# An AdaLN block with attention and routed LoRA experts: a VectorE order, a TensorE order, and the second half of the FFN in float16 pairs

## What is computed

```python
h = _layernorm(x) * (1 + ca) + sa
x = x + ga * attention(h, Wq, Wk, Wv, Wo)
h = _layernorm(x) * (1 + cb) + sb
top_w, top_i = top_k(h @ gate_w.T, 2);  routing = softmax(top_w)
# for every expert e, with its weight w_e per token:
h1 = h @ w1.T + h @ A1.T @ B1.T * 2;  h3 = h @ w3.T + h @ A3.T @ B3.T * 2
act = silu(h1) * h3
out += w_e * (act @ w2.T + act @ A2.T @ B2.T * 2)
x = x + gb * out
```

## Time and profile before

| | us |
|---|---|
| median of 3 runs | 527.52 |
| the profiled execution's own time | 527.2 |
| its span, first to last instruction | 525.2 |
| mean granted TensorE clock | 0.987 of 2.4 GHz |
| TensorE busy | 467.9 (89%) |
| VectorE / ScalarE / GpSimd busy | 355.4 / 331.5 / 278.2 |

### The profile page before, as it was taken

One profiled execution on the slowest core, in us unless ns is written; L12 is line 12 of the kernel. 1 busy time (PEld: TensorE's weight loads), 2 busy tenths in 40 slices (PEclk: granted clock), 3 DMA queues, 4 the chain that ended last, 5 costly groups with the idle time before them and its releaser, 6 DMA issues.

```text
span 525.2 us, 11947 instructions
## 1 busy us (share of the span) xinstructions
PE 467.9 (89%) x4424; PEld 320.3 (61%) x4424; DVE 355.4 (68%) x1016; ACT 331.5 (63%) x592; POOL 278.2 (53%) x208
## 2 busy tenths in 40 slices
PE   3777789989999999999999988989798979999996
PEld 3363566667767677777677766767663534564444
DVE  3686667777777778777878887888648746424442
ACT  3417889888789878888888889797435443001110
POOL 4136698894779875769999557631103204001110
PEclk9978999999999999999999999999999989999999
DMA  8156043394352584343536413342110000010001
GB/s 302 49 143 217 24 130 94 119 222 93 102 89 64 163 149 117 99 74 110 168 87 141 112 21 112 101 116 41 21 21 1 1 0 1 0 41 1 0 2 40
DMA packets 58169, 44.47 MB, mean 85 GB/s; under 512 B 36608, under 2 KB 50432, under 8 KB 58112
## 3 DMA queue, kind: packets, MB, share of 16 engines
q1 hardware_dynamic: 56624, 41.60, 31.3%
q10 hardware_dynamic: 1488, 2.10, 1.1%
HBM read 23.77 MB, written 11.53 MB: 67 GB/s over the span
## 4 chain that ended last, share of the span: by engine, by line
PE 65%; DVE 12%; ACT 11%; issue 7%; POOL 2%; DMA 1%; SPq 0%; ACTq 0%; DVEq 0%; POOLq 0%
PE ps L463 10%; PE ps L389 8%; PE ps L391 8%; PE ps L390 8%; ACT prob L777 6%; PE ps L714 4%; PE ps L481 4%; PE ps L447 4%; PE ps L445 4%; PE ps L485 4%; PE ps L483 4%; PE ps L652 3%; PE ps L642 3%; DVE pl L1061 2%; ACT rot L756 1%
## 5 line engine op out<-in xcount | busy, mean ns | idle before, releaser
L777 ACT ACTIVATE prob<-prob,least 128x512 f32<-128x512 f32 (+3 forms) x256 | 131.5, 551 | 0.0
L1053 DVE CUSTOM_DVE_ANT_0 prob<-ps,causal 128x512 f32<-128x512 f32 (+3 forms) x256 | 114.3, 484 | 4.9 <-PE ps L447 4.3
L463 PE MATMUL ps<-ident,prob 128*128 128x128 f32 x640 | 93.4, 279 | 23.2 <-ACT prob L777 18.6
L784 ACT ACTIVATE ph<-ps 128x512 f16<-128x512 f32 (+1 forms) x128 | 89.5, 700 | 28.4 <-PE ps L463 25.0
L1061 DVE SCALAR_TENSOR_TENSOR pl<-ps,ph 128x512 f16<-128x512 f32 (+1 forms) x128 | 99.0, 815 | 0.0
L463 PEld LDWEIGHTS ps<-ident,prob 128*128 128x128 f32 x640 | 67.8, 141 | 38.0 <-ACT prob L777 25.7
L445 PE MATMUL ps<-kT_h,qT 128*128 128x512 f16 (+3 forms) x256 | 76.6, 300 | 4.5 <-DVE least L1053 2.9
L1314 POOL TENSOR_TENSOR on_l<-on,on_h 128x512 f16<-128x512 f32 x32 | 37.1, 1160 | 63.6 <-ACT on_h L791 63.6
L447 PE MATMUL ps<-kT_l,qT 128*128 128x512 f16 (+3 forms) x256 | 69.8, 300 | 0.0
L481 PE MATMUL ps<-vh,ph 128*128 128x65 f16 x640 | 64.9, 194 | 0.9 <-DVE pl L1061 0.9
L483 PE MATMUL ps<-vl,ph 128*128 128x64 f16 x640 | 64.9, 193 | 0.0
(11 more groups left out here) (156 smaller groups left out, 951.8 us busy)
## 6 DMA issues: line engine op xcount, KB each, us to landing
spill<-rot SPq DMA_DIRECT2D x20, 512.0 KB, 3.4
qT<-spill SPq DMA_DIRECT2D x16, 512.0 KB, 3.6
wst<-chunks SPq DMA_DIRECT2D x30, 256.0 KB, 3.9
kT_h<-spill SPq DMA_DIRECT2D x8, 256.0 KB, 4.0
oT<-wmod ACTq DMA_DIRECT2D x3, 512.0 KB, 11.4
kT_l<-spill SPq DMA_DIRECT2D x4, 256.0 KB, 4.8
out<-xs SPq DMA_DIRECT2D x4, 256.0 KB, 2.1
w_h<-w2T SPq DMA_DIRECT2D x1, 640.0 KB, 6.1
```

The costliest lines, as they stand in the source:

```text
L463: mm = pe.transpose(ps[:, PT_BANK + c // 512, c % 512:c % 512 + P], prob[:, m % 2, c:c + P], ident[:, :])
L777: act.activation(prob[:, m % 2, c], prob[:, m % 2, c], ACT.Exp, bias=least[:, m % 2, qt:qt + 1], scale=-1.0).then_inc(exp_done, 1)
L1053: ins = dve.tensor_tensor_reduce(prob[:, m % 2, at:at + w], ps[:, bank, off:off + w], causal[:, S - w:S], -1.0 / HD ** 0.5, 3.0e38, ALU.ad ...
```

## The change

Attention, per period:
- VectorE does `probs_low(n+1, 0)` before `norm(n)` instead of behind `row_max` 2; part 1 stays last.
- TensorE does `scores(n+3, 0)` before the output product and before the second projection step; group 1 stays last.

FFN:
- A2, w2 and B2 come as five float32 chunks of 512 columns (period 54, into `raw` and `rot`), and are split like the other weights: five ScalarE copies in periods 57 to 61 (`late_high`), five GpSimd subtractions one period later (`late_low`).
- `z_product` becomes three float16 matmuls per tile and choice, one tile later; ScalarE rounds `av` (`products_high`), GpSimd makes the remainder (`products_low`; the last one is VectorE's). `av` gets two slots.
- `gsum` is rounded by ScalarE (`sums_high`), its remainder made by GpSimd (`sums_low`); w2 and B2 products are three float16 matmuls each. In batch 0 the w2 products stand behind tile 5 of batch 0, their B2 part in tile 1 of batch 1; in batch 1 two thirds of the w2 products stand before the last `z_product`.
- ScalarE takes SiLU of the next tile's first choice before it rounds the second product of this one.
- The masks' PSUM banks alternate (`i % 2`).
- Batch 1: the residual moves to GpSimd in four pieces, the inverse root and the normalisation to GpSimd, the transposes from tile 1 to tile 2, logits from 1 to 3, choices, weights and masks a tile or more later.

```diff
                 if n == 54:
-                    sp.wait_ge(proj_done, len(TILES))
-                    ... four DMAs: a2, w2
+                    lowered(sp, len(ITEMS) - 1)
+                    for i in range(LATE_CHUNKS):
+                        sp.dma_start(late_stage(i), chunks[N_CHUNKS + i]).then_inc(ld_late, 16)
 # TensorE, period n
+                if n + 3 < HEADS:
+                    scores(n + 3, 0)
                 if n >= 10 and n % 2 == 0:
...
                     output((n - 10) // 8, (n - 10) % 8 // 2, out_bank(n))
                 for step in steps[1:]:
                     project(step)
-                for f in range(2):
-                    if n + 3 < HEADS:
-                        scores(n + 3, f)
+                if n + 3 < HEADS:
+                    scores(n + 3, 1)
 # VectorE, period n
+                if 0 <= n + 1 < HEADS:
+                    probs_low(n + 1, 0)
                 if n >= 0:
                     norm(n)
...
                 if 0 <= n + 1 < HEADS:
-                    probs_low(n + 1, 0)
                     probs_low(n + 1, 1)
 # TensorE, FFN
-                mm = pe.matmul(ps[:, 4 + s, :], a2_sb[0:m, f, :], av[0:m, s, :], start=(f == 0), stop=(f == FT - 1))
+                    mm = mm3(ps[:, 4 + s, :], a2_h[0:m, f, :], a2_l[0:m, f, :], av_h[0:m, i % 2, s, :], av_l[0:m, i % 2, s, :],
+                             f == 0, f == FT - 1)
+            def w2_product(b, t, f):
+                m, at = min(P, F - f * P), t % 2 * D
+                pe.wait_ge(fs["gl"], b * FT + f + 1)
+                for l, r in ((gsum_h, w2_h), (gsum_h, w2_l), (gsum_l, w2_h)):
+                    mm = pe.matmul(ps[:, 6 + t // 2, at:at + D], l[0:m, f, c], r[0:m, f, :], ...)
+            def b2_product(b, t):
+                pe.wait_ge(fs["ul"], 1 if b == 0 else 2 + t // 2)
+                for l, r in ((u_h, b2_h), (u_h, b2_l), (u_l, b2_h)):
...
             for b in range(B):
                 for f in range(FT):
                     if f < FT - 1:
                         if b > 0 or f > 0:
                             h_base(b, f + 1)
-                        h_lora(b, f + 1)
-                        if b == 0 and f == 1:
+                            h_lora(b, f + 1)
+                        if b == 0 and f == 2:
                             pe.wait_ge(op_added, 4 * W + 4)
                             ... transposes of batch 1
+                        if b == 0 and f == 3:
+                            gate_logits(1)
                     elif b == 0:
                         h_base(1, 0)
-                        h_lora(1, 0)
+                    else:
+                        pe.wait_ge(fs["og"], 2)
+                        w2_products(1, (0, 1))
                     h_second(b, f)
+                    if b == 0 and f == 4:
+                        mask_transposes(1, (0, 1))
                     if f > 0:
-                        z_product(b, f - 1, 1)
-                    z_product(b, f, 0)
+                        z_product(b, f - 1)
+                    if b == 1 and f == 1:
+                        for t in range(T):
+                            b2_product(0, t)
...
+                w2_products(b, (2, 3))
+                z_product(b, FT - 1)
+                w2_products(b, (4, 5))
 # ScalarE, FFN, tile i
+                if i > 0:
+                    sums_high(i - 1)
+                if i == 1:
+                    root(1, B + 2)
+                products_high(i, 0)
+                if i == 2:
+                    modulate_ffn(1, 6)
...
+                silu(i, 1)
+                if i < B * FT - 1:
+                    silu(i + 1, 0)
+                products_high(i, 1)
 # GpSimd, FFN, tile i
+                products_low(i, 0)
                 if i == 1:
+                    inverse_root(1)
+                    for t in range(T):
+                        normalise(1, t)
+                sums(i)
+                if i < B * FT - 1:
+                    products_low(i, 1)
...
+                sums_low(i)
```

365 lines of the change are left out of this document (222 added, 143 removed).

## The result

| | before | after |
|---|---|---|
| median, us | 527.94 (4 runs) | 519.57 (4 runs) |
| ratio, 95% interval | | 0.9857, 0.9828 to 0.9886 |
| the profiled execution's own time | 527.2 | 520.1 |
| its span | 525.2 | 518.2 |
| mean granted clock | 0.987 | 0.972 |

The changed kernel is faster by 1.4% by the ratio (about 7.5 us), by 8.4 us by the medians; the forecast was 515.4 us, 4.2 us less. The time lies in the forecast's range of 508.5 to 521.5 us, but the gain is under the 2% that it called a clear one, and for which it gave 0.62. (One of the four runs of before, 563.66 us, was disturbed and is left out of the ratio.)

What follows compares the result with a forecast made beforehand. TensorE was taken as the main bound, busy 467.9 of 525.2 us, with ScalarE's queue and later VectorE among the heads. 527.2 + 1.0 (attention) - 6.9 (batch 0) - 6.9 (batch 1) + 1.0 (end) = 515.4 us, range 508.5 to 521.5.

Steps and rivals of the forecast that it cites:

- Heads, VectorE's order: Attention: the low part moved ahead of the normalisation shortens TensorE's waits for `pl` from 310 us on, -3.3 us.
- (a): Attention, periods 50, 52, 54, 56: the moved scores fill TensorE's output-product waits for the normalisation, -1.7 us.
- (b): Attention, periods 3, 7, ..., 47: scores between two steps of one tile cost 0.43 us each of twelve times, +5.2 us.
- Rival A: Attention: the path through period 35 has unseen slack, so (b) costs nothing, 510.2 us; chance 0.25.
- (c): Attention: output products end 0.43 us later; VectorE's idle time hides it, uncovered up to 0.43 us per odd period.
- Late weights: Attention, periods 57 to 61: five ScalarE roundings ahead of the tile-1 exponential cost a quarter of 3.1 us, +0.8 us.
- FFN, matmul time: FFN, both batches: float16 z products -5.2 us, w2 and B2 products -9.0 us, together -14.2 us.
- FFN, batch 0's waits: FFN of batch 0: TensorE's idle stretches in the new order sum to 9.4 us instead of 7.1, +2.3 us.
- The clock dip: FFN of batch 0: half of the 1.6 us lost at the low clock is given back, -0.8 us.
- B: FFN of batch 0: GpSimd's and ScalarE's queues hold TensorE 4 us more, with a second dip 520.5 us; chance 0.15.
- D: FFN, both batches: removed matmul time returns as uncovered waits, 522.5 us with half given back; chance 0.10.
- C: FFN: GpSimd becomes the bound, deciding from 7.5 us a tile, at worst +35, 550 us; chance 0.05.

Runs made afterwards that it cites:

- experiment 1: Three edits of the changed kernel that undo or restrict its new orders among the heads: attn_old 518.05 us, dve_old 521.86 us, pe_even 512.62 us.
- pe_even: Changed kernel with the first half of the scores ahead of the output product in even periods only, in odd ones behind the projection step: 512.62 us, ratio 0.9735.
- dve_old: Changed kernel with only VectorE's order among the heads put back, both low parts behind the normalisation: 521.86 us, ratio 0.9914.
- attn_old: Changed kernel with both TensorE's and VectorE's order among the heads put back, late weights and FFN as changed: 518.05 us, ratio 0.9847.
- best_late: best with ScalarE's late-weight roundings behind the tile-1 exponential instead of ahead of it in periods 57 to 61: 505.52 us, ratio 0.9602.
- experiment 2: Cost of low-clock stretches: changed kernel with zero-adding matmuls in three TensorE waits of batch 0, 520.58 us; the changed kernel unedited again, 519.18 us.
- experiment 4: Changed kernel with GpSimd subtracting batch 1's product remainders twice or three times instead of once: 524.88 and 538.04 us.
- best: pe_even plus two ScalarE/VectorE reorderings in batch 0, an early four-column SiLU, and product (4,0) ahead of batch 1's second choice: 506.78 us, ratio 0.9635.
- after_again: The changed kernel run once more, unedited: 519.18 us.

## Why the prediction was right or wrong

**Heads, VectorE's order (-3.3):** right, about -3.1 by experiment 1 (-2.6 and -0.6), with some luck in where. The low part fits ahead of the normalisation. Behind 310 us, where the forecast saw all of the gain, it was about 2 us; the rest came before that, 0.48 us each in periods 1 and 9. TensorE's waits there (one line of before, 310 to 376 us, then two after the change, 310 to 374):

```profile
PEld ps L463 <- ACT prob L777: 2.7, 3, 1.2
```
```profile
PEld ps L480 <- ACT prob L830: 5.4, 5, 1.8
...
PEld ps L480 <- DVE pl L1154: 0.8, 2, 0.6
```

The waits for `pl`, 5.4 us over 11 times in the earlier trace rows, are nearly gone, and waits for exponentials took the place of a part of them, as forecast. VectorE's waits for the values gave way to waits for the high parts (`pl` behind `ph`: 19.3 us, 15 times, from 100 to 250 us), as idle time that costs nothing.

**Heads, TensorE's order:** (a) the filled output waits, -1.7, were -1.7 in the four periods named. Another -1.4 us of small gains had no term. (b) the scores between two steps of a tile, +0.43 in each of twelve periods, were 0.43 in each against pe_even (0.39 net against before). The size was right, the count was not: periods -1 and 0 grew in the same way, by 0.53 and 0.43 us (dve_old against before), and were not in it. That is +1.0, so +6.1 in all. Rival A, that (b) costs nothing, is refuted by pe_even. One sentence in the forecast was wrong in its wording: the wait of the last two transposes isn't longer, TensorE itself is later. (c), up to 0.43 us in odd periods, cost nothing: they take 4.39 to 4.40 us in attn_old and dve_old alike from 29 to 37.

**Late weights (+0.8):** +0.5 with the orders of before, in period 58 alone. With the new orders they stood in the path of periods 60 and 62 too; moving them in best_late gained 1.3 us.

**Heads in all:** without low stretches the terms measured give -3.1 - 1.7 - 1.4 + 6.1 + 0.5 = +0.4, where +1.0 was forecast. The other 2.6 of the +3.0 are the two low stretches before 85 us (2.8 us, experiment 2), less a start that came 0.2 us earlier. The forecast had no term for them, since the trace of before showed none there.

**FFN, matmul time:** -14.2 forecast. In batch 0, among kernels with one low stretch as before had, busy time went from 82.2 to 73.3 us, -8.9 for -8.4. z products stand 0.65 us apart, and w2 with B2 takes 9.5 us for 9.2. In batch 1 it went from 52.6 to 46.7, -5.9 for -5.8: the difference was right, but the stretch was forecast from a sum of its own, 45.5 us, and that sum was 1.2 us short, as matmul groups don't join without gaps (w2 8.3 us for 7.9, a tile now and then 6.69 us for 6.48). With 0.97 us idle for the 1.0 forecast, this mis-sized sum is the whole 1.1 us of the miss in batch 1. Taking less the difference would have given 47.8 us; it was 47.6.

**FFN, batch 0's waits (+2.3):** the list came to 9.4 us; the idle time is 8.2 with three low stretches and 10.7 with one, as before had, so +3.6 for +2.3. The longest wait, ahead of `h_base(0, 4)`, was forecast at 3.3 and was 2.86, ended by VectorE behind a SiLU, as written; 2.3 behind the first `h_second` was 2.13. What failed is one item above all, 0.6 us "while VectorE makes the choices": it was 2.3 to 2.5. VectorE in the second choice, after the change:

```profile
434.58 1.26 DVE L1219 TENSOR_TENSOR fsm<-fsm,fs 128x32 f32<-128x32 f32 x1
435.88 1.08 DVE L1221 TENSOR_TENSOR fsm<-fsm,rev 128x32 f32<-128x32 f32 x1
436.99 0.18 DVE L1223 TENSOR_REDUCE fs<-fsm 128x4 f32<-128x32 f32 x1
437.21 0.86 DVE L1225 TENSOR_TENSOR fsm<-fsm,fs 128x32 f32<-128x32 f32 x1
```

The three with two SBUF inputs take 0.19 us elsewhere; here each ends 0.05 us behind a GpSimd operation (experiment 4), and the reduction, with one input, stays short. Product (4,0) stood behind them all. best, which moves that product ahead, has this wait no more, and 0.98 us ahead of the mask transposes behind it. Two smaller items offset each other: the list had nothing ahead of `h_base(0, 5)`, where dve_old and after_again wait for 1.2 us, and 1.9 us for the masks, which are 0.3 or less in after and dve_old and 1.8 in attn_old.

**The clock dip (-0.8):** wrong in kind. It was counted as lost time to be had back. It came three times instead of once, and 2.5 of the 3.0 us more of busy time that this makes were taken from idle time. Batch 0 is 84.0 to 84.5 us with one, two or three of them.

**Rivals.** B, a longer chain in batch 0 and a second dip, is nearest to what happened, 520.5 us against 519.6, though its size isn't right: the stage's idle time at one low stretch was 1.3 us longer than forecast, not 4, and the further dips cost 0.2 to 0.3 us each there, not 1.6. Its reason, small VectorE work that waits for GpSimd, is what made the choices long. D in its weak form holds for batch 0, where 8.9 us of matmul time gave a gain of 4.8 us. C was refuted as a fact (no z product waited for GpSimd), but its threshold was wrong too: it decides from 6.5 us a tile, not 7.5, and the slack is 1.4 us a tile. The lower end of the range, 508.5, is 508.1 by the terms it names (510.2 less 2.1).

**End (+1.0):** +0.6. Four VectorE steps stand there, and both stores begin behind the second and the fourth.

## To carry over

A piece of work of one engine may fill a wait of its own, but not stand ahead of a result that another engine returns to it: there it cost its full length every time, however small, and pe_even got about 6 us back by moving 0.43 us of scores. Where a stage is a chain over four engines, take matmul time out of it last: measure busy and idle time of the stage in several kernels, and if one falls as the other rises, look for the chain behind the waits, and shorten that. Forecast a stretch as its old row less the difference, not as a new sum of parts.
